# Scatters that read a copy of the row numbers, and a last expert whose outer layer ends row tile by row tile

## The reference

```python
E, K, CF, D, H = 8, 2, 1.2, 512, 2048
cap = ceil(CF * N / E)                                    # 4096 tokens: 615 rows for each expert
probs = softmax(x @ Wr + br);  gates, ids = top_k(probs, K)
# each expert keeps its cap strongest (token, gate) pairs: disp_tok, disp_g
xg = x[disp_tok].reshape(E, cap, D)                       # gather
h = silu(einsum('ecd,edh->ech', xg, W1) + b1)             # inner layer, 512 -> 2048
out = einsum('ech,ehd->ecd', h, W2) + b2                  # outer layer, 2048 -> 512
y = zeros.at[disp_tok].add(out * disp_g)                  # scatter with addition
```

## Time and profile before

| | us |
|---|---|
| median of three executions | 2804.74 (2800.78, 2804.74, 2806.18) |
| the profiled execution, its own time | 2798.69 |
| its span, first to last instruction | 2797.1 |
| PE busy / DVE / ACT / POOL in the span | 2482.8 / 1555.9 / 1215.7 / 649.9 |
| PE busy in the stretch 1962 to 2772 (experts 1 to 7) | 797.41 of 810.00 |

### The profile page before, as it was taken

How to read it: one execution, slowest core, us unless ns; L and a number is a source line. 1 busy time by engine, 2 the same in 40 slices (tenths; PEclk the granted TensorE clock), 3 DMA queues, 4 the chain that set the end, 5 groups by cost and what they waited for, 6 DMA issues and landing times. The chain is left out here.

```text
span 2797.1 us, 48481 instructions
## 1 busy us (share of the span) xinstructions
PE 2482.8 (89%) x17245; PEld 2196.9 (79%) x17245; DVE 1555.9 (56%) x2545; ACT 1215.7 (43%) x1908; POOL 649.9 (23%) x1037
## 2 busy tenths in 40 slices
PE   5999999999994699999999984269999999999996
PEld 4899999999983577777777773158888888888885
DVE  6788787887873356565656653744343343333431
ACT  5565555655551244444444442024343343434442
POOL 1111111111112344343534431120311203113011
PEclk9899999999996799999999997579999999999998
DMA  3110100101003566665555542122433424333221
GB/s 108 32 33 24 46 24 28 42 24 46 25 17 105 152 163 166 169 165 160 158 163 163 164 128 95 41 67 67 125 86 106 99 71 124 80 113 94 83 64 19
DMA packets 232201, 254.31 MB, mean 91 GB/s; under 512 B 68264, under 2 KB 158376, under 8 KB 231440
## 3 DMA queue, kind: packets, MB, share of 16 engines
q1 hardware_dynamic: 190992, 231.17, 28.3%
q0 software_dynamic: 40960, 20.41, 4.1%
HBM read 182.47 MB, written 68.80 MB: 90 GB/s over the span
## 5 line engine op out<-in xcount | busy, mean ns | idle before, releaser
L1790 PE MATMUL d_psH<-d_xgT_h,d_w_l 128*128 128x308 f32 x1024 | 318.2, 311 | 5.6 <-issue 4.2
L303 PE MATMUL a_psP<-a_xnT_h,a_win_l 128*128 128x256 f32 x1024 | 305.5, 298 | 15.5 <-DVE a_xnT_l L540 14.4
L2015 DVE TENSOR_TENSOR d_h_l<-d_hf,d_h_h 128x616 fp32r<-128x616 f32 x128 | 102.1, 800 | 383.3 <-ACT d_h_h L1859 383.3
L1791 PE MATMUL d_psH<-d_xgT_l,d_w_h 128*128 128x308 f32 x1024 | 314.5, 307 | 0.0
L1792 PE MATMUL d_psH<-d_xgT_h,d_w_h 128*128 128x308 f32 x1024 | 313.8, 306 | 0.0
L1892 ACT ACTIVATE d_hf<-d_psH,d_b1c 128x308 f32<-128x308 f32 x256 | 130.8, 517 | 409.1 <-PE d_psH L1792 409.1
L304 PE MATMUL a_psP<-a_xnT_l,a_win_h 128*128 128x256 f32 x1024 | 296.6, 290 | 0.0
L305 PE MATMUL a_psP<-a_xnT_h,a_win_h 128*128 128x256 f32 x1024 | 295.8, 289 | 0.0
L1790 PE MATMUL d_psO<-d_w_h,d_h_l 128*123 128x512 f32 x640 | 253.2, 396 | 8.0 <-DVE d_h_l L2015 8.0
L1755 POOL DMA_INDIRECT out_dram<-d_ob,d_ids x40 | 103.7, 2592 | 650.4 <-ACT d_ob L1909 640.7
L1791 PE MATMUL d_psO<-d_w_l,d_h_h 128*123 128x512 f32 x640 | 253.3, 396 | 0.0
(11 more groups left out here) (314 smaller groups left out, 6206.0 us busy)
## 6 DMA issues: line engine op xcount, KB each, us to landing
d_w<-in_W_dram SPq DMA_DIRECT2D x64, 1024.0 KB, 7.2
b_qst<-qs_d SPq DMA_DIRECT2D x48, 512.0 KB, 6.5
b_kst<-ks_d SPq DMA_DIRECT2D x48, 512.0 KB, 6.7
a_xl<-in_x_dram SPq DMA_DIRECT2D x16, 512.0 KB, 4.3
a_xres<-in_x_dram SPq DMA_DIRECT2D x16, 512.0 KB, 3.8
x_d<-a_xres SPq DMA_DIRECT2D x16, 512.0 KB, 3.1
b_xa<-x_d SPq DMA_DIRECT2D x16, 512.0 KB, 10.0
b_cx<-in_ctxT_dram SPq DMA_DIRECT2D x16, 512.0 KB, 9.1
```

The lines of the kernel that those rows point to most:

```text
L303: pe.matmul(out, lo_w, hi_x, start=first, stop=False)
L1790: pe.matmul(out, lo_w, hi_x, start=first, stop=False)
L1791: pe.matmul(out, hi_w, lo_x, start=False, stop=False)
L2015: dve.tensor_tensor(out, a, b_, ALU.subtract).then_inc(done, 1)
```

## The change

Scatters read their row numbers from a new tile `to`. At the end of each body DVE waits until the scatters of the expert before have landed, copies `ids` into `to` (L2129 of the changed kernel) and signals `to_s`, for which POOL waits. `lists` loses its wait on `sc`. In the last expert, the inner tiles 12 to 15 are "held": their high and low parts go into the four column planes of `xgT_h[0]` and `xgT_l[0]`, which no later expert needs, `outer` is not called for them inside the loop, and `outer_held` multiplies them at the end with the row tile as the outer loop.

```diff
+        to = sb("to", [R, NT], I32)
...
+        def held(e, m):
+            return last(e) and m >= MH - MC
+
+        def hidden(e, m):
+            if held(e, m):
+                return xgT_h[0][:, m - (MH - MC), :], xgT_l[0][:, m - (MH - MC), :]
+            return h_h[:, m % 2, :], h_l[:, m % 2, :]
...
                 wait(pool, sc, 16 * NT * e)
                 g.sem_inc(passed_p, 1)
+                pool.wait_ge(to_s, e + 1)
+                g.sem_inc(passed_p, 1)
                 for t in range(NT):
                     pool.wait_ge(og_s, NT * e + t + 1)
...
-                    g.indirect_dma_start(out=y, out_offset=bass.IndirectOffsetOnAxis(ap=ids[par][:, t:t + 1], axis=0),
+                    g.indirect_dma_start(out=y, out_offset=bass.IndirectOffsetOnAxis(ap=to[:, t:t + 1], axis=0),
...
+                def outer_held():
+                    pe.wait_ge(w2_lo, CH * e + CH)
+                    for t in range(NT):
+                        for m in range(MH - MC, MH):
+                            if t == 0:
+                                pe.wait_ge(h_lo, MH * e + m + 1)
+                            mm = outer_tile(m, t)
                         mm.then_inc(o_mm, 1)
...
-                    if m:
+                    if m and not held(e, m - 1):
                         outer(m - 1)
...
-                outer(MH - 1)
+                if last(e):
+                    outer_held()
+                else:
+                    outer(MH - 1)
...
-                    if m >= 2:
+                    if m >= 2 and not held(e, m):
                         act.wait_ge(o_mm, OM * e + m - 1)
...
-                    copy(h_h[:, m % 2, :], hf[:, m % 2, :], h_hi)
+                    copy(hidden(e, m)[0], hf[:, m % 2, :], h_hi)
...
             def lists(e, par):
-                wait(dve, sc, 16 * NT * (e - 1))
                 wait(dve, og_s, NT * (e - 1))
...
-                    minus(h_l[:, m % 2, :], hf[:, m % 2, :], f32(h_h[:, m % 2, :]), h_lo)
+                    hh, hl = hidden(e, m)
+                    minus(hl, hf[:, m % 2, :], f32(hh), h_lo)
...
+                wait(dve, sc, 16 * NT * e)
+                dve.sem_inc(passed_v, 1)
+                dve.tensor_copy(to[:], ids[par][:]).then_inc(to_s, 1)
                 for t in range(NT):
-                    dve.wait_ge(o_mm, OM * e + MH - 1 + t + 1)
-
-                    wait(dve, sc, 16 * NT * e)
+                    dve.wait_ge(o_mm, OM * e + (MH - MC if last(e) else MH - 1) + t + 1)
                     dve.tensor_tensor(ob[:, t, :], psO[t][0:R, :], b2r[par][:], ALU.add).then_inc(ob_s, 1)
```

More of the change, by code:

```diff
@@ L1559, in experts_phase @@
         h_mm, silu_s, h_hi, h_lo, o_mm = sem("h_mm"), sem("silu"), sem("h_hi"), sem("h_lo"), sem("o_mm")
-        ob_s, og_s, sc = sem("ob"), sem("og"), sem("sc")
+        ob_s, og_s, to_s, sc = sem("ob"), sem("og"), sem("to"), sem("sc")
         w1_v = W1.rearrange("e (k p) h -> e p k h", p=P)
@@ L1817, in body, with outer_tile @@
                 pe.wait_ge(g_lo, NT * (e + 1))
+                def outer_tile(m, t):
+                    s_ = (m // MC) % 2
+                    cc = slice(t * R, (t + 1) * R)
+                    hh, hl = hidden(e, m)
+                    return split_mm(psO[t][0:R, :], hh[:, cc], hl[:, cc], w2_h[s_][:, m % MC, :],
+                                    w2_l[s_][:, m % MC, :], m == 0, m == MH - 1)
                 def outer(m):
-                    c, s_ = m // MC, (m // MC) % 2
                     pe.wait_ge(h_lo, MH * e + m + 1)
-                    pe.wait_ge(w2_lo, CH * e + c + 1)
+                    pe.wait_ge(w2_lo, CH * e + m // MC + 1)
                     for t in range(NT):
@@ L1826, in outer @@
                             wait(pe, ob_s, NT * (e - 1) + t + 1)
-                        cc = slice(t * R, (t + 1) * R)
-                        mm = split_mm(psO[t][0:R, :], h_h[:, m % 2, cc], h_l[:, m % 2, cc], w2_h[s_][:, m % MC, :],
-                                      w2_l[s_][:, m % MC, :], m == 0, m == MH - 1)
+                        mm = outer_tile(m, t)
                         if m == MH - 1:
@@ L1832, in outer @@
                     if m < MH - 1 :
+                        mm.then_inc(o_mm, 1)
+                def outer_held():
[4 more added lines that the diff above has]
+                                pe.wait_ge(h_lo, MH * e + m + 1)
+                            mm = outer_tile(m, t)
                         mm.then_inc(o_mm, 1)
@@ L1894, in body @@
                     act.wait_ge(silu_s, 2 * (MH * e + m + 1))
-                    if m >= 2:
+                    if m >= 2 and not held(e, m):
                         act.wait_ge(o_mm, OM * e + m - 1)
-                    else:
+                    elif m < 2:
                         wait(act, o_mm, OM * e)
-                    copy(h_h[:, m % 2, :], hf[:, m % 2, :], h_hi)
+                    copy(hidden(e, m)[0], hf[:, m % 2, :], h_hi)
                     if m >= 5 and (m - 5) % 2 == 0 and (m - 5) // 2 < NT and not last(e):
```

## The result

| | before | changed |
|---|---|---|
| median, us | 2805.11 (2800.78 to 2806.18, 4 runs) | 2786.47 (2782.04 to 2789.45, 4 runs) |
| the profiled execution, us | 2798.69 | 2782.04 |
| its span, us | 2797.1 | 2780.4 |

The ratio is 0.9931, 95% interval 0.9913 to 0.9949: 18.6 us less, where 18.5 were forecast (the time was forecast at 2785).

What follows compares the result with a forecast made beforehand. PE was taken to bound the experts until about 2772, then the chain of five scatters on POOL; 10.4 + 8.1 = 18.5 us off the middle of earlier executions, taken as 2785, range 2776 to 2796.

Steps and rivals of the forecast that it cites:

- Part 1: Experts' stretch: without the list's wait for scatters, PE's four waits for `h_l` go; 8.0 + 0.7 + 1.7 = 10.4 us.
- my 8.0: Experts 1 to 7: total of PE's four waits for DVE's `h_l`, all forecast to go, 8.0 us.
- my 1.7: After the pause in expert 4: time lost at the lower clock, forecast to be won back, 1.7 us, plus or minus 2.
- the falls behind the loop's turn stay: At the loop's turn: the pauses, 4.2 us, and the clock's fall after one were to stay; no gain counted.
- Rival D: PE's clock: pauses fall otherwise, two or three more lower it, 1.7 us each; time 2790, chance 0.08.
- rival E: Inner tile 5: earlier gathers fall among scatters and weight loads, PE waits for gathered rows; slower, 2815, chance 0.03.
- rival B: Inner tile 3: PE's waits stay or return as DVE finds the list's matmuls or ACT late; 2795, chance 0.09.
- a slack of PE: Experts' stretch: PE's slack was said to hide two of DVE's six waits, which give nothing when removed.
- Part 2: End of each body: eight DVE copies and the new waits fit into idle time; cost 0, without that cover 1.3 us.
- Part 3: Last expert: held inner tiles, multiplied row tile by row tile, bring first and last scatter 8.1 us sooner.
- rival C: Last expert's outer matmuls: twelve in a row into one bank run slower, costing 10 us; time 2795, chance 0.03.
- head start: Last expert's scatters: POOL's first start, 1.0 us behind `ob`, lets it keep its own beat; without it 7.7 us, not 8.1.

## Why the prediction was right, and where it was not

**Part 1, the list without its wait, was right in its mechanism and too small.** 10.4 was forecast. Three looped traces with the wait have six bodies of 698.0, 699.6 and 702.3 us (mean 700.0); six looped traces without it have 682.2 to 686.8 (mean 683.9). That is 16.0, or 5.6 more than forecast.

PE's waits were 8.0, 8.7 and 10.5, mean 9.1 against my 8.0: 1.1 of the 5.6. The first matmul after each wait starts 0.33 ahead of the next one instead of 0.23, which I left out: 0.4. The loop's pauses are 4.8 us with the wait and 4.5 without: 0.3.

The largest part is the clock. With the wait the bodies spent 10.2, 10.2 and 13.6 us at the lower level, without it 0 to 6.8 (mean 2.8). At most half of the difference, 4.3, is lost time (inner matmuls start 0.26 apart there instead of 0.14), against my 1.7. In the first trace the lower level stood at three places, each just behind a pause: the loop's turn, the wait in expert 4, the loop's turn again (us, PE busy, clock, DMA share, GB/s):

```profile
2199.00:2200.00 1.00, 1.00 (x6) 0.50 0.50 93
2345.00:2346.00 1.00, 1.00 (x4) 0.50 0.06 5
2434.00:2435.00 1.00, 1.00 (x6) 0.50 0.46 113
```

Behind PE's waits for `h_l` there were 3.4, 0 and 6.8 us of it in the three traces, mean 3.4, which is the 1.7 lost that I had. The term that was off is another: I wrote that the falls behind the loop's turn stay. With the wait the clock fell at all six turns of three traces, 6.8, 10.2 and 6.8 us; without it at only five of twelve, 2.8 on average. That is up to 2.6 us lost less. The pauses at the turns are hardly shorter without it (4.5 us in total against 4.8), so either the waits made the falls at the turns more likely or it is chance; no run here decides. Rival D, more falls than before, did not come.

Together these are 4.4 of the 5.6; for the other 1.2 I have no row. In the written-out pair, one trace each, the sum closes: the waits 13.5, 6 x 0.17 for the modelled ends, 6 x 0.1 for the matmuls behind them and at most half of 10.2 for the clock are 20.2, and the bodies differ by 19.8 (697.5 and 677.7).

That the clock's share varies between executions is what the Trainium skill's rule on free-running windows led me to carry as plus or minus 2 ("TensorE: Matmul & The Clock Gate", "What's actually happening"). The traces agree with the rule: with the loop's pauses of 3.8 to 5.5 us in total, the same bodies had 0, 3.4 or 6.8 us at the lower level, and without pauses none. The step that failed was to take the size of such a term, and that a part of it stays, from one trace.

**Its side steps held.** The gathers moved up and no PE row waits for them: rival E falls. Nothing else is late at inner tile 3 but the list's matmuls, 2.3 us at most, which PE does not feel: rival B falls. The two DVE waits that cost PE nothing were covered by the loop's turn, not by a slack of PE as I wrote; written out, they cost as the others do.

**Part 2** costs nothing: the copy takes 0.17 us and DVE is idle 0.96 behind it.

**Part 3, held tiles, was right to a tenth.** 8.1 was forecast for the first scatter; the last expert takes 102.41 instead of 110.49, in both traces of the changed kernel: 8.08. The inner tiles 12 to 15 in a row made PE wait nowhere but the 0.28 us at the tenth matmul. Outer matmuls of one bank in a row start 0.23 apart: rival C falls. The end as a whole is 138.1 in four traces without held tiles and 130.1 in four with four held, also 8.1. Two small errors hide in that. First, POOL does not keep its 2.70. I counted the 1.0 us between `ob` and its start as a head start; it is paid at each scatter anew, so PE sets 2.77 (0.3 in all, the 7.7 that I had named for no head start). Second, the time from the last scatter's start to the span's end, which I took as fixed, is 13.6 to 14.9 us without held tiles and 13.5 to 14.7 with four, so no trace is good for less than about 1 us there.

**The total.** The parts as the traces have them are 16.0 and 8.1, together 24, against 18.5 forecast. The measured ratios allow 14 to 24 us in the first measurement and 17 to 28 in the second, so the runs agree with either; if the change costs 2.5 us ahead of the experts, which is not shown, the whole is some 21.6. That the forecast time of 2785 met the 2786.47 so closely is in part luck. With 16.0 for part 1 the same working would have said about 2779, and medians of four executions wander by some us: the changed kernel's ten executions reach from 2780.8 to 2792.0.

## What to carry to other kernels

A wait stands for everything queued behind it. Here a buffer of 20 bytes a partition, kept until slow transfers had landed, held back the engine that feeds TensorE, and a copy of those bytes took 0.17 us. (No run here shows up to when a scatter reads its row numbers, so whether the wait had to be for the landing at all is untested.) Ask of each wait how long the resource is kept by its slowest reader, and whether that reader can have its own copy.

When a program ends in a chain behind the bounding engine, reorder the last stretch of that engine so that its results come out one by one, no faster than the chain's slowest step takes them (2.70 here). With three held, 2.1 us of PE a row tile, POOL fell behind and started its last scatter 5.4 us after PE's last matmul. With four (2.8) and six (4.2) it was 2.9, so a slower pace than needed cost nothing.

Compare traces by stretches between fixed instructions, not by spans; and take a term that comes and goes, as the clock does, from several traces.

## What the runs showed of the hardware

- A turn of the loop of two bodies pauses PE 1.6 to 3.8 us (nine looped traces, two turns each), written-out bodies pause 0 (three traces).
- Pauses of PE of 1.0 to 3.8 us can be followed by a stretch at the lower clock, and equal ones are not always: 10.2 to 13.6 us of it in the looped bodies with six pauses, 0 to 6.8 in those with two, none in those without.
- POOL starts a scatter 1.0 us after the last data it waits for is ready (ACT's end at 2754.79, start at 2755.79), even where it has idled only 0.37 us.
- The middle scatters of a sequence land sooner when spaced wider (8.3 to 9.4 us at 4.15 apart, 10.2 to 11.2 at 2.70). The last one is the slowest either way (11.7, and 12.7 to 14.1), whatever its rows.
